# An attention stage on eight cores: the mixed inputs of two projections formed one product earlier, in a second buffer, and a sigmoid evaluated in place in PSUM

## What is computed

```python
x  = layernorm(x)
xx = shift_by_one_token(x)
xk = x * time_mix_k + xx * (1 - time_mix_k)      # the same for v and r
k, v, r = xk @ W_key.T, xv @ W_value.T, xr @ W_receptance.T
sr = sigmoid(r)
# per channel, in order of time, with w = -exp(time_decay), u = time_first:
#   y_t = (p + exp(u + k_t) * v_t) / (q + exp(u + k_t))
#   p   = exp(w) * p + exp(k_t) * v_t
#   q   = exp(w) * q + exp(k_t)
out = (sr * y) @ W_output.T                      # added to the residual
```

## Time and profile before

| | us |
|---|---|
| median of 3 runs | 2991.97 |
| lowest of them | 2991.05 |
| the profiled execution | 2991.09 |
| its span, slowest core (core 7) | 2989.5 |
| spans of the eight cores | 2983.2 to 2989.5 |

### The profile page before, as it was taken

How to read it: one execution, slowest core, us unless ns; L and a number is a source line. 1 busy time by engine, 2 the same in 40 slices (tenths; PEclk the granted TensorE clock), 3 DMA queues, 4 the chain that set the end, 5 groups by cost and what they waited for, 6 DMA issues and landing times.

```text
span 2989.5 us, 21628 instructions; the slowest of 8 cores (2983.2 to 2989.5 us)
## 1 busy us (share of the span) xinstructions
PE 1873.9 (63%) x7648; PEld 784.3 (26%) x7648; DVE 1278.7 (43%) x1772; ACT 330.1 (11%) x551; POOL 67.9 (2%) x88
## 2 busy tenths in 40 slices
PE   2405404503602267888888788788788788788785
PEld 1102101201201033333333333333333333333332
DVE  4464454455445653224424434434434434334333
ACT  0220230130040000010010010010000000000000
POOL 0000000000001000000000000000000000000000
PEclk8656757756856678989889889899889889889897
DMA  6502401411304400003213213213213213203102
GB/s 146 80 0 57 76 9 28 67 18 28 56 0 61 67 16 7 1 3 47 36 16 49 36 15 50 35 15 50 35 15 50 36 15 50 36 15 50 29 1 113
DMA packets 69195, 112.79 MB, mean 38 GB/s; under 512 B 2480, under 2 KB 37312, under 8 KB 68048
## 3 DMA queue, kind: packets, MB, share of 16 engines
q0 software_dynamic: 63856, 94.50, 20.9%
q1 hardware_dynamic: 5232, 16.91, 1.7%
HBM read 197.28 MB, written 8.52 MB: 69 GB/s over the span
## 4 chain that ended last, share of the span: by engine, by line
PE 50%; DVE 9%; issue 2%; ACT 1%; DVEq 0%; DMA 0%; ACTq 0%; POOLq 0%
PE pc L639 17%; PE pc L665 15%; PE pc L653 14%; DVE h L708 4%; DVE sg L707 4%; PE pc L604 2%; PE pc L623 1%; ACT sg L737 1%; PE pc L612 1%; DVE acc L681 1%; DVE h L678 1%; DVE acc L716 0%; DVE h L690 0%; DVEq L36 0%; DMA cb<-comb_dram 0%
## 5 line engine op out<-in xcount | busy, mean ns | idle before, releaser
L639 PE MATMUL pc<-ln2x,wsl 128*128 128x512 bf16 x1920 | 521.6, 439 | 191.0 <-ACT sg L737 190.0
L665 PE MATMUL pc<-h,wsl 128*128 128x512 bf16 x1920 | 461.3, 404 | 101.6 <-DVE h L708 100.6
L707 DVE TENSOR_TENSOR sg<-sg,pc 128x512 f32<-128x512 f32 x240 | 165.0, 687 | 824.6 <-PE pc L653 805.3
L653 PE MATMUL pc<-ln2x,wsl 128*128 128x512 bf16 x1920 | 427.6, 379 | 0.0
L716 DVE TENSOR_TENSOR acc<-acc,pc 128x512 f32<-128x512 f32 x480 | 330.0, 688 | 183.4 <-PE pc L665 144.3
L639 PEld LDWEIGHTS pc<-ln2x,wsl 128*128 128x128 bf16 x1920 | 206.7, 110 | 504.8 <-issue 345.3
L339 PE MATMUL pb<-mx,wsla 128*128 128x512 bf16 x768 | 195.6, 422 | 208.9 <-DVE mx L219 100.3
L737 ACT ACTIVATE sg<-pc 128x512 f32<-128x512 f32 x240 | 143.4, 597 | 1525.0 <-PE pc L639 1018.4
L339 PE MATMUL pb<-sry,wsla 128*128 128x512 bf16 x256 | 64.9, 421 | 383.0 <-DVE sry L258 383.0
L665 PEld LDWEIGHTS pc<-h,wsl 128*128 128x128 bf16 x1920 | 190.2, 102 | 372.7 <-issue 192.6
L653 PEld LDWEIGHTS pc<-ln2x,wsl 128*128 128x128 bf16 x1920 | 187.6, 98 | 230.2
(11 more groups left out here) (116 smaller groups left out, 825.5 us busy)
## 6 DMA issues: line engine op xcount, KB each, us to landing
wsl<-gw POOLq DMA_DIRECT2D x15, 1024.0 KB, 9.5
wsl<-uw POOLq DMA_DIRECT2D x15, 1024.0 KB, 10.2
wsl<-dw POOLq DMA_DIRECT2D x15, 1024.0 KB, 10.6
acc<-x SPq DMA_DIRECT2D x4, 2048.0 KB, 24.2
wsla<-wk POOLq DMA_DIRECT2D x4, 2048.0 KB, 16.8
wsla<-wv POOLq DMA_DIRECT2D x4, 2048.0 KB, 18.5
wsla<-wr POOLq DMA_DIRECT2D x4, 2048.0 KB, 16.5
wsla<-wo POOLq DMA_DIRECT2D x4, 2048.0 KB, 16.5
```

Of the source, the lines that this page charges most:

```text
L639: inst = t.matmul(pc4[tc][:], slot_ap(3 * e)[:, kc, ocI * 128:(ocI + 1) * 128], ln2x[:, kc, 2 + tc * 512: 2 + (tc + 1) * 512], start=(kc = ...
L653: inst = t.matmul(pc4[4 + tc][:], slot_ap(3 * e + 1)[:, kc, ocI * 128:(ocI + 1) * 128], ln2x[:, kc, 2 + tc * 512: 2 + (tc + 1) * 512], sta ...
L665: inst = t.matmul(pc4[(oc % 2) * 4 + tc][:], slot_ap(3 * e + 2)[:, kcI, oc * 128:(oc + 1) * 128], h[:, kcI, tc * 512:(tc + 1) * 512], star ...
L707: VS.do(lambda sl=sl, tc=tc: v.tensor_tensor(sl[:], sl[:], pc4[4 + tc][:], OP.mult))
```

## The change

1. A second buffer for a mixed input, `mxb`, is added. The eight instructions of mixv now write `mxb` and stand right behind mixk, ahead of the wait for K.
2. The eight instructions of mixr (still into `mx`) move from behind vevac to ahead of the wait for V.
3. PE reads `mxb` in product V (`rhs_t`). Its waits are the same ones by name.
4. The sigmoid keeps its three instructions for each bank, but all of them read PSUM and the first two write it, in place, where `tB` stood in SBUF. The mark `sigread`, after which PE may write the banks again, moves from the first exponential of the last bank to the last one.
5. `tB` and `ev_t` go away; `w1` takes the place of `ev_t`.

```diff
+            mxb = e1(nc.sbuf_tensor("mxb", [128, CC, SCW], BF16))
...
-            tB = e1(nc.sbuf_tensor("tB", [128, SCW], F32))
...
-            ev_t = e1(nc.sbuf_tensor("ev_t", [128, CC, L], F32))
...
                     VS.ms[f"v:mixk{s_}"] = VS.v
+                    for cc in range(CC):
+                        VS.do(lambda cc=cc: v.scalar_tensor_tensor(
+                            mxb[:, cc, :], xsq[:, cc, :], TMV(cc), ln1x[:, cc, 0:SCW], OP.mult, OP.add))
+                    VS.ms[f"v:mixv{s_}"] = VS.v
                     v.wait_ge(s_pe, MS(f"t:MAT{4 * s_ + 0}"))
                     for od in range(CC):
                         VS.do(lambda od=od: v.tensor_copy(k_sb[:, od, :], pb[od][:]))
                     VS.ms[f"v:kevac{s_}"] = VS.v
                     for cc in range(CC):
                         VS.do(lambda cc=cc: v.scalar_tensor_tensor(
-                            mx[:, cc, :], xsq[:, cc, :], TMV(cc), ln1x[:, cc, 0:SCW], OP.mult, OP.add))
-                    VS.ms[f"v:mixv{s_}"] = VS.v
+                            mx[:, cc, :], xsq[:, cc, :], TMR(cc), ln1x[:, cc, 0:SCW], OP.mult, OP.add))
+                    VS.ms[f"v:mixr{s_}"] = VS.v
                     v.wait_ge(s_pe, MS(f"t:MAT{4 * s_ + 1}"))
                     for od in range(CC):
                         VS.do(lambda od=od: v.tensor_copy(v_sb[:, od, :], pb[od][:]))
                     VS.ms[f"v:vevac{s_}"] = VS.v
-                    for cc in range(CC):
-                        VS.do(lambda cc=cc: v.scalar_tensor_tensor(
-                            mx[:, cc, :], xsq[:, cc, :], TMR(cc), ln1x[:, cc, 0:SCW], OP.mult, OP.add))
-                    VS.ms[f"v:mixr{s_}"] = VS.v
...
-                        VS.do(lambda ksl=ksl: v.tensor_tensor(ev_t[:], e_t[:], v_sb[:, :, ksl], OP.mult))
+                        VS.do(lambda ksl=ksl: v.tensor_tensor(w1[:], e_t[:], v_sb[:, :, ksl], OP.mult))
...
-                        SS.do(lambda od=od: s.activation(tB[:], pb[od][:], AF.Exp, scale=-1.0),
+                        SS.do(lambda od=od: s.activation(pb[od][:], pb[od][:], AF.Exp, scale=-1.0))
+                        SS.do(lambda od=od: s.activation(pb[od][:], pb[od][:], AF.Ln, bias=1.0))
+                        SS.do(lambda od=od: s.activation(srl[:, od, :], pb[od][:], AF.Exp, scale=-1.0),
                               f"sigread_{s_}" if od == CC - 1 else None)
-                        SS.do(lambda: s.activation(tB[:], tB[:], AF.Ln, bias=1.0))
-                        SS.do(lambda od=od: s.activation(srl[:, od, :], tB[:], AF.Exp, scale=-1.0))
...
-                        rhs_t = sry if mi == 3 else mx
+                        rhs_t = (mx, mxb, mx, sry)[mi]
```

More of the change, by code:

```diff
@@ L247, in _ @@
                             VS.do(lambda cc=cc: v.tensor_tensor_scan(
-                                P_ch[:, cc, 1:], ewb[:, cc, :], ev_t[:, cc, :],
+                                P_ch[:, cc, 1:], ewb[:, cc, :], w1[:, cc, :],
                                 P_ch[:, cc, 0:1], OP.mult, OP.add))
```

## The result

The changed kernel took 2942.69 us in the median of its 10 runs (2933.25 to 3090.18), the kernel before beside it 2992.6 (2991.05 to 3245.16). The ratio of the undisturbed runs is 0.9824, with a 95% interval of 0.9811 to 0.9837: 1.8% less. That is 50 us of the 58 that the sum gave, and 3.7 us above the range.

A forecast was written before the change was run, and what follows sets the result against it. Engines almost take turns, with both mixes on the chain between products while PE waits. Four slabs x (6.85 + 6.85 + 0.77) = 57.9 us saved gives 2934 us from the 2991.97 median; range 2929 to 2939.

The forecast's parts named there:

- the sum: Over four slabs of the attention block: 6.85 + 6.85 + 0.77 us saved in each, 57.9 us together, giving 2934 us.
- The gaps: PE's waits before products V and R: 13.53 us each shrinks to 6.68, saving 6.85 us twice a slab.
- The cover: Moved mixes run beside products K and V, 6.85 us each, with 9.3 and 9.8 us to spare.
- The sigmoid: Behind R on ACT: a bank's three instructions take 582, 582 and 597 ns, saving 0.77 us a slab.
- The clock across the gap: Rival at V and R: clock stays up across the gap, saving 21 us in all, 2913 us; chance 0.02.
- The weights of R: Rival before R: its weight load lands after the 30.0 us now allowed, making the kernel slower, 3052 us; chance 0.02.
- The good luck: Rival in V and R: the clock rises favourably, two products at 15.25 instead of 16.7 us, giving 2931; chance 0.40.
- The clock: On PE's products: starts at 0.50, granted 1.00 some time in; luck of the rise allowed 3 us either way over four slabs.
- It moves a product by 1.5 us at most: On PE's products: luck in where the clock rises changes one product's length by 1.5 us at most.
- The rivals: Four alternatives: good clock luck (0.40), clock staying up across the gap (0.02), mixes slowed beside products (0.02), late R weights (0.02).
- The stages behind the same length: After the attention block, the stages behind 931 us keep their length and are only shifted.

## Why the prediction was right and wrong

**Right.** *The gaps.* 6.68 us forecast, 6.57 measured, eight times. *The cover.* The mixes take 751 ns beside a product as alone; DVE's idle time before kevac is 9.36 us as forecast (9.5). *The sigmoid.* 582, 582 and 597 ns. *The clock across the gap.* V and R start at 0.50, so it did not stay up. *The weights of R.* No wait for them in the changed kernel; the load lands in 17.6 us by the median, of the 30 allowed. *The sum.* Core 5, free of 0.81 in both traces, went from 2987.5 to 2930.1: 57.4 us against 57.9. Over the four slabs it saved 61.7 us and behind them it lost 4.1, so that the agreement to 0.5 us is in part luck. *The good luck.* Part of the surplus is the case that the prediction gave 0.40: R in its short form. On core 5 it took 15.3 to 15.4 us in all four slabs after the change, and 16.8 to 16.9 in all four before; O gave some of it back. Left alone, the kernel is at 2930.7 to 2932.7 us in three sittings, where 2934 was forecast. (The three lowest runs of the first, 2933.3 to 2935.1, have a core or two above 2931 us and may hold an occurrence; they have no traces.)

**Wrong.** The measured 2942.69 lies above the range of 2929 to 2939. The step that failed is *The clock*: it took the clock to have the two values that the rows of before show, and allowed 3 us for when it rises. A third one, 0.81, took 3.6 us an occurrence, three times on the slowest core: 10.9 us, beside an allowance of 3. "It moves a product by 1.5 us at most" failed with it: O took 18.39 us against 16.60. The rivals had four ways to go and none for a limit that the change may call up, though more matmuls in less time is just what it does. The page of the Trainium skill named above has the value; no row of before shows it, and the trace of before has none. With it as a rival (three slabs x 3.6 us on the slowest pair, 2945) the range would have held.

**The moved stages.** "The stages behind the same length" held within what the cores differ by themselves. Core 5 took 2054.7 us from O to the end before and 2058.8 after, but the eight cores of before lie at 2054.8 to 2058.1 and those of after at 2055.8 to 2059.9, the mean 1.7 us higher. An allowance of 3 us for luck in the attention block leaves out this spread, in 2000 us that the change does not touch.

**Open.** Why the raised pairs come in one sitting and not in another, on the same chip even; why a pair of cores in some executions and the whole die in others, and whether it depends on which stages of the pairs fall together; whether both short gaps are needed for the full occurrence. That the shorter gaps have a part in it rests on one sitting with kernels side by side, and is supported by the first; how is not settled.

## What to carry to other kernels

When one engine's work stands between two products of another, ask which of it needs the first product. What does not goes ahead of the wait, with a buffer of its own if the old one is still being read, and the gain is the gap's, instruction by instruction. Then hand over by bank, not by product: it gave another 4.3% here, until a weight load became the wait. And where a change packs matmuls more closely on all cores, price a clock of 0.81 for the third product and the one behind it (3.6 us for the two here), and measure in more than one sitting before believing a difference of 10 us.

## What the runs showed of the hardware that was not expected

- A granted clock of 0.81 in the third of three products 6.57 us apart, 7 to 10 us after its start, which came back at O with 95 us of an idle PE between, and was gone at the next K, 165 us after it had come. The two cores of a pair get it within 0.2 us.
- In executions with a whole die raised, stretches of 0.81 on the two pairs lie at one constant distance by the cores' own times (2230.54 and 1874.73 us in two profiles): one event on four cores whose pairs began that far apart. Where pairs are raised alone, no one distance fits.
- The same kernel on the same chip had it in 5 of 5 executions at one time and in none of this form in 6 at another.
- With products back to back, V starts at 1.00 and takes 13.98 us where no other limit holds it, and the stretches of 0.81 that came (2.4 to 6.4 us) had no visible cost.
- Small savings don't add up to the microsecond: the sigmoid's 3.1 us measured as 5 alone and as nothing on top of the mixes, and part of the difference is that each new spacing meets the rise of the clock at another point (O at 16.23 and 16.61 us).
